# A six-block decoder on one core: normalised target by ScalarE, values' tile cleared at the begin of the matrix memory, target's copy behind the memory's logarithm

## The reference

```
x = LN(x + attention_0(x))            # 16 heads, with decay tables and a logarithm of the scores
x = LN(x + matrix_memory(x, ctx))     # 8 heads: gates, cumulative sums, D = exp(...), C = qk * D
x = LN(x + experts_0(x))              # shared MLP + top 2 of 8 experts, tokens sorted by expert
x = LN(x + attention_1(x))            # 16 heads of 8 channels
x = LN(x + mix(x, ctx))               # two projections
x = LN(x + experts_1(x))              # shared MLP + 8 gated experts
```

## Time and profile before

| | us |
|---|---|
| median of 3 runs (lowest to highest) | 2300.03 (2291.24 to 2302.69) |
| the profiled execution, its own time | 2291.94 |
| its span, from the first to the last instruction | 2290.1 |
| PE, DVE, ACT, POOL busy | 1903.2, 1672.3, 1120.7, 843.9 |
| mean granted TensorE clock | 0.916 of full speed |

### The profile page before, as it was taken

The page is one execution under the profiler, slowest core; times in us unless marked ns, Lnnn a source line. Parts: engine busy times, 40 slices in busy tenths (PEclk is TensorE's granted clock), DMA queues, the critical chain, the costliest instruction groups (busy, mean ns, idle before and its releaser), DMA issues.

```text
span 2290.1 us, 39869 instructions
## 1 busy us (share of the span) xinstructions
PE 1903.2 (83%) x14136; PEld 1361.8 (59%) x14136; DVE 1672.3 (73%) x4099; ACT 1120.7 (49%) x3181; POOL 843.9 (37%) x766
## 2 busy tenths in 40 slices
PE   3885698888897898788897898788897889787798
PEld 2564367755685567655685567646684568565464
DVE  8986895679847894679747994789667994735355
ACT  5561366436652556336642566346643565244343
POOL 1551463327512662327421651337431751311000
PEclk8997899989997999889997999899997999788799
DMA  4000011302040012202040012101040203233000
GB/s 147 1 1 10 14 61 30 108 10 75 1 130 18 18 58 79 59 10 74 6 127 15 27 48 88 50 22 63 6 132 11 74 1 119 92 100 102 10 15 24
DMA packets 72491, 116.56 MB, mean 51 GB/s; under 512 B 7822, under 2 KB 46870, under 8 KB 71782
## 3 DMA queue, kind: packets, MB, share of 16 engines
q1 hardware_dynamic: 66758, 100.90, 13.8%
q0 software_dynamic: 5536, 13.12, 1.9%
HBM read 94.66 MB, written 18.28 MB: 49 GB/s over the span
## 4 chain that ended last, share of the span: by engine, by line
DVE 38%; PE 36%; issue 12%; POOL 5%; ACT 5%; DMA 2%; SPq 1%; DVEq 0%; POOLq 0%; ACTq 0%
PE bank L1515 33%; DVE work L516 12%; DVE bank L525 5%; DVE work L514 4%; ACT work L1048 3%; DVE work L534 3%; POOL hid L1416 2%; DVE max L831 2%; PE bank L1519 1%; DVE norm_t_st L446 1%; POOL work L1396 1%; DVE norm_x_st L446 1%; DMA hid<-y_sorted,slot_id 1%; DVE acc L737 1%; POOL work L1391 1%
## 5 line engine op out<-in xcount | busy, mean ns | idle before, releaser
L1515 PEld LDWEIGHTS bank<-work 128*128 128x128 f32 (+2 forms) x5152 | 388.7, 200 | 170.7 <-issue 163.8
L1515 PE MATMUL bank<-work 128*128 128x128 f32 (+2 forms) x5152 | 420.6, 308 | 53.1 <-DMA work<-in_wo 25.2
L1048 ACT ACTIVATE work<-bank 128x512 f32<-128x512 f32 (+1 forms) x560 | 247.0, 519 | 295.7 <-PE bank L1515 263.7
L516 DVE TENSOR_TENSOR work<-bank,table_space 64x512 f32<-64x512 f32 x512 | 352.2, 688 | 6.8
L1384 POOL TENSOR_TENSOR work<-work 128x512 f32<-128x512 f32 x128 | 163.6, 1278 | 398.2 <-PE bank L1515 319.4
L1048 ACT ACTIVATE work<-work 128x512 f32<-128x512 f32 (+1 forms) x338 | 196.6, 618 | 119.0 <-DVE work L604 81.0
L1048 ACT ACTIVATE work<-work,negmax 128x128 f32<-128x128 f32 x512 | 199.1, 390 | 99.6 <-DVE negmax L536 99.6
L1391 POOL TENSOR_TENSOR work<-sb_ident,nrm 128x512 f32<-128x512 f32 x128 | 133.3, 1041 | 201.3 <-ACT nrm L1048 200.5
L1048 ACT ACTIVATE hid<-bank,w_ring 128x128 f32<-128x128 f32 x480 | 136.4, 370 | 132.5 <-PE bank L1515 132.4
L1515 PE MATMUL bank<-work,table_space 128*128 128x512 f32 x256 | 140.5, 630 | 65.9 <-DVE negmax L536 58.0
L514 DVE TENSOR_TENSOR work<-bank,table_space 128x512 f32<-128x512 f32 x256 | 173.7, 678 | 27.0 <-PE bank L1515 21.4
(11 more groups left out here) (296 smaller groups left out, 3378.3 us busy)
## 6 DMA issues: line engine op xcount, KB each, us to landing
w_ring<-in_w_routed SPq DMA_DIRECT2D x120, 514.0 KB, 4.6
x_quad<-x_sorted SPq DMA_DIRECT2D x24, 256.0 KB, 2.9
y_sorted<-y_quad SPq DMA_DIRECT2D x24, 256.0 KB, 4.3
x_T<-in_x_T POOLq DMA_DIRECT2D x9, 256.0 KB, 3.2
x_row<-in_x_row POOLq DMA_DIRECT2D x9, 256.0 KB, 3.8
ctx_T<-in_ctx_T SPq DMA_DIRECT2D x8, 256.0 KB, 2.7
work<-in_ctx_row SPq DMA_DIRECT2D x8, 256.0 KB, 3.0
out<-act_row SPq DMA_DIRECT2D x8, 256.0 KB, 2.3
```

What stands on the lines that cost most here:

```text
L516: last = v.tensor_tensor(rows(wk[i + 1][o]), rows(src[p]), sinT[o, s].unsqueeze(1).broadcast_to([DH0, GB, N]), ALU.mult)
L1048: return nc.scalar.activation(o, i, f, **k)
L1515: return nc.tensor.matmul(o, l, r, start=start, stop=stop, skip_group_check=True)
```

## The change

Three edits, all in `xattn` with `d` = 1:

- The target is normalised by ACT instead of DVE. DVE makes `centre0 = -mean * rstd` between two steps of the denominator; ACT waits for it (and for the earlier store from `act_row[0]`, a wait that stood on DVE) and writes `act_row[0]` with four `Identity` instructions.
- ACT's copy of the transposed target to `seq_T` goes from ahead of the memory's first logarithm and exponential to behind them.
- POOL clears `v2` at the begin of `xattn`, ahead of its waits for the context and the gates, instead of behind the last gather.

```
+        centre0, centred0 = sb("centre0", 128, GB), sem("centred0")
...
# DVE, xattn
                 link(v.tensor_tensor(den[:], rden[:], eM[:], ALU.max))
+                if d:
+                    dve.wait_ge(norm_t.ready, g * LNS + 1)
+                    v.scalar_tensor_tensor(centre0[:], norm_t.mv[:, :, 0], -1.0, norm_t.rstd[:], ALU.mult,
+                                           ALU.mult).then_inc(centred0, 1)
                 link(v.tensor_scalar(den[:], den[:], 1.0e-6, None, ALU.add))
                 link(v.reciprocal(rden[:], den[:]))
-                if d:
-                    dve.wait_ge(stored, g * 32 + 16)
-                    norm_apply(norm_t, g, 0, acc, act_row[0])
...
# ACT, xattn
                 if d:
                     norm(norm_t, g, 0)
-                    t_to_T(g, 0, bank[6])
+                    act.wait_ge(stored, g * 32 + 16)
+                    act.wait_ge(centred0, g + 1)
+                    for b in range(GB):
+                        last = fn(act_row[0][:, b], acc[:, b], ACT.Identity, bias=centre0[:, b:b + 1],
+                                  scale=norm_t.rstd[:, b:b + 1])
+                    last.then_inc(norm_t.out, 1)
                 norm(norm_x, g, 1, ahead=d)
                 if d:
+                    t_to_T(g, 0, bank[6])
                     mask_k2(g)
...
# POOL, xattn
+                if d:
+                    q.memset(work[:, 18 * W:22 * W], 0.0).then_inc(v2_clear, 1)
                 pool.wait_ge(in_ctx, tally(g, d, 32, 32))
                 pool.wait_ge(gate_max, tally(g, d, 1, 1))
...
-                if d:
-                    q.memset(work[:, 18 * W:22 * W], 0.0).then_inc(v2_clear, 1)
                 pool.wait_ge(norm_x.out, tally(g, d, LNS, 3))
```

## The result

The changed kernel is slower: a median of 2324.58 us in 4 runs (2321.46 to 2326.11) against 2295.64 in 4 runs of the kernel before (2284.45 to 2302.69), a ratio of 1.0129 with an interval of [1.0082, 1.0175]. The forecast of 2311.0 has the right sign, but the time lies 3.6 us above the top of its range, 2321.0. The profiled execution took 2321.46 us, 29.5 more than that of before (2291.94), and the difference lies inside the span.

A forecast was written before the change was run, and what follows sets the result against it. No single engine was taken to bound the kernel, but chains of waits around each edit. The sum was 2291.94 + 0 + 11.0 = 2302.9, with the 8.09 shift 2311.0 us; range 2293.5 to 2321.

The forecast's parts named there:

- Target by ScalarE, copy behind the logarithm: 0: Memory's end: DVE's 0.95 us gain ends in a new wait; both edits together 0, bounds -1.4 to +2.1 us.
- within 0.1: Sign to look for: ACT's four `Identity` end where DVE's L456 had ended, within 0.1 us.
- DVE's gain arrives whole: Rival at the memory's end: ACT's masks done in time, 7 x 0.95 = 6.7 us go, 2293.4 with no hold; chance 0.07.
- Clearing at the begin: held: At the inverse root, POOL's clearing holds DVE's `tensor_scalar` L469 until the clearing's end plus 0.04 us, 1.57 us.
- the three answers: DVE beside POOL: two inputs held (L664), two inputs not held beside a clearing (L737), SBUF-to-SBUF at double rate not shown.
- the two bounds, 0 and 1.57 us: Delay of L469 in the inverse root: 0 as for L737, or 1.57 us if held until the clearing's end.
- double rate: DVE working SBUF to SBUF: `tensor_scalar` at 128x512 takes 420 ns, against 722 ns out of a bank; L469 may be such.
- Which instruction, and for how long: 1.57: L469, second step of DVE's inverse root, starting 0.12 us behind the clearing's begin, is held from 399.65 to 401.22.
- everything on the chain from `row_x` on is 1.57 us later: 7 x 1.57 = 11.0 us: With L469 held, its delay reaches PE's transposes and all behind them in each of seven periods, 11.0 us in all.
- Held, and the clock falls too: Rival behind PE's longer wait: half a clock fall in all seven periods, 10.5 us more, 2321.5; held cases together 0.54.
- The shift of 8.09 us: Median of the runs shown, 2300.03, minus the profiled 2291.94; added to the sum at the end.

The follow-up runs named there:

- e2: The changed kernel with POOL's clearing put back behind the last gather, leaving only the first two edits; 0.9988 of the kernel before, median 2295.82 us.
- e10: The kernel before with the first edit alone: target by four `Identity` on ACT, `centre0` on DVE; 1.0000 of the kernel before, median 2291.81 us.
- e8: e4 with ACT's last logarithm and exponential of the memory moved behind the first of four key masks; 0.9948 of the kernel before, median 2286.24 us.
- e9: e2 with ACT's last logarithm and exponential of the memory ahead of three of the four key masks; 0.9969 of the kernel before, median 2286.03 us.
- e4: The changed kernel with the inverse root's two `tensor_scalar` replaced by forms with a second SBUF input; 0.9973 of the kernel before, median 2290.76 us.
- e3: The changed kernel with the clearing held until DVE has normalised `row_x`, still ahead of the gates; 0.9998 of the kernel before, median 2297.61 us.
- e6: The kernel before, clearing untouched, with an extra DVE memset of 128x1640 ahead of the inverse root in seven periods; 1.0102, median 2319.79 us.
- e7: The changed kernel with two unread 128x512 matmuls on PE ahead of its wait for `row_x` in seven periods; 1.0048 of before, median 2307.78 us.
- e5: The changed kernel with half the tile cleared at the begin and half behind the last gather; 0.9987 of the kernel before, median 2292.89 us.
- e1: The kernel before with the third edit alone, POOL's clearing at the begin of the matrix memory; 1.0093 of the kernel before, median 2319.04 us.

## Why the prediction was right or wrong, point by point

- **Target by ScalarE, copy behind the logarithm: 0.** Right (`e2` 0.9988, `e10` 1.0000), and for the reason given: DVE's gain ends in a wait for ACT, at the masks in `e2` and already at the copy in `e10`. Two sizes were off. The four `Identity` take 1.65 us instead of 1.50 (the four of the earlier trace rows read a bank and these read `acc`, which I had not noticed; whether that is why, no run shows) and start 0.37 behind the root instead of 0.24, so the target is out 2.02 us behind the root's end (450.98 - 448.96) where DVE had it after 1.76; "within 0.1" missed by 0.16, and by the zero of the sum nothing hung on it.
- **DVE's gain arrives whole.** It did not. `e8` and `e9` show what it lacked: the masks out of the logarithm's way; then 0.5 to 0.7 of the 0.95 us arrive.
- **Clearing at the begin: held.** Right: the third of the three answers that the trace of before left open. I had chosen it between the two bounds, 0 and 1.57 us; no row of before decided it. `e4` tells it from the other two, since two SBUF inputs are not held beside a clearing (L737, 0.29 us each) and a `tensor_scalar` is, at four elements too: beside a clearing of the same size `tensor_scalar` took 1.93 us instead of 0.16, copy 2.03 (`e3`) instead of 0.42, and the two-input forms 0.15 and 0.16 (`e4`). What I called double rate is, at 128x512 from SBUF to SBUF in the trace of before, 420 ns for the `tensor_scalar` of L839 and 417 for the copy of L551, against 692 for the two inputs of L641. That the hold comes with this rate was my estimate: the held forms are the faster ones at that size, and no run shows more. One point stays open. Here the held L469 is recorded 0.04 to 0.07 us ahead of the clearing in all seven periods, too close to tell from these records which of the two was first.
- **Which instruction, and for how long: 1.57.** Undersized. I had L469 of before start 0.12 us behind the clearing, and took the end of POOL's load (399.36) for the clearing's begin. The clearing was recorded some 0.04 ahead of the load's recorded end (651.25, with 650.70 + 0.59 = 651.29), beside the *first* `tensor_scalar`, which ran from 399.28 to 399.44, across the begin that I had assumed, and which I did not consider. It is held until the clearing ends: 1.77 us more a period, 12.4 us instead of 11.0.
- **The step that failed: "everything on the chain from `row_x` on is 1.57 us later: 7 x 1.57 = 11.0 us".** It took the price of DVE's lateness to be its length, and put the fall of the clock behind it at nothing. In all seven periods the matmuls behind the longer wait ran for 3.4 us at the lower clock, and the stage took 1.63 us more in each, 11.4 us in all. I had that case as the rival "Held, and the clock falls too", with 1.5 a period and 2321.5 us, and by my own chances it had 0.30 of the 0.54 for a held clearing; yet the sum left it out, because I took PE's dense work beside the transposes for a sign against it. The 1.5 was half of an estimate of 3.0 for a whole fall: 255.90 us between two clearings against 252.90 a period earlier, with a stretch at 0.66 in the longer one where the other had 1.00. No run shows that term; in its place the runs showed 1.63 us a period in the change and 1.62 in `e6`. The work behind the wait is dense (PE busy 3.90 of 4 us in the kernel before); it was the stillness ahead that counted, as `e6` (late without POOL: 1.0102) and `e7` (as late, with PE kept at work: 1.0048) show.
- **The sum with the measured sizes:** 23.8 us on 2295.64 makes 2319.4, a ratio of 1.0104, inside the measured interval. The 5 us from there to the median of 2324.58 stay open: in the one trace of each kernel the other stages differ with their clock falls, which vary between periods of either kernel, and four runs don't settle whether the change adds to them.
- **The base.** The shift of 8.09 us rested on three runs; with a fourth the median of before is 2295.64. That made the forecast 4.4 us higher and hid part of the miss.

## What to carry to other kernels

Before you move "free" work of an idle engine, look at which instructions of the other engines it will run beside, and in which form: here a 0.16 us instruction on the chain became 1.93 us, and a form with a second SBUF input, or a place one step later, cost nothing. Price a wait of PE with the clock behind it, above all where the trace shows PE standing still for next to nothing now: 1.77 us more cost 3.4 (0.92 us more, in `e5`, brought no fall), and two products that nobody reads gave 1.6 of them back. Where two paths meet at one engine within a tenth of a microsecond, shorten both or reorder that engine's queue; one path alone gave under 0.1 us a period.

## What the hardware showed that I had not expected

- A clearing by POOL, which reads nothing, holds a DVE instruction of four elements for all of its length: 1.93 us beside 1.85, 1.08 beside 1.00.
- The held instruction was recorded some 0.05 us before the clearing in all seven periods: a start ahead of POOL's in the records is no sign that an instruction will pass unheld.
- With 0.92 us more of lateness (`e5`) the clock behind the wait did not fall in any of seven periods; with 1.77 and 1.84 (`e6`, and the change) it fell in all seven, and in `e1`, with 1.77, in six of seven. Why the one period of `e1` kept its clock is not shown.
- The clock's falls in the later stages are not the same from one trace to the next of kernels with equal work there, and move a period by 3 us; this may be why the 6.4 us of `e5` were not seen, but no run shows it.
